# A graph-attention layer whose residual is added in DRAM by accumulating transfers from Pool

## The reference

```
h = jnp.maximum(_layernorm(x, axis=-1), 0.0)
...
h_src = h[src]
h_tgt = h[tgt]
att_in = jnp.concatenate([h_src, h_tgt, e], axis=-1)
att = jnp.sum(att_in * a, axis=-1)
att = jnp.where(att > 0, att, 0.2 * att)
m = jnp.maximum(segment_max(att, tgt), 0.0)
ex = jnp.exp(att - m[tgt])
denom = segment_sum(ex, tgt) + (num_edges - deg)[:, None] * jnp.exp(-m)
h_prime = segment_sum((ex / denom[tgt])[:, :, None] * h_src, tgt)
...
x = x + h_prime
```

## Time and profile before

| | |
|---|---|
| median of 3 runs | 2291.24 us (2289.3 to 2291.45) |
| the profiled execution: its time | 2286.65 us |
| the profiled execution: its span | 2284.8 us |
| Pool busy | 1676.3 us (73%) |
| VectorE busy | 1597.1 us (70%) |
| TensorE busy (matmul) | 1208.8 us (53%) |
| ScalarE busy | 602.1 us (26%) |
| transfers | 199.98 MB, mean 88 GB/s |

### The profile page before, as it was taken

How to read it: one execution, slowest core, us unless ns; L and a number is a source line. 1 busy time by engine, 2 the same in 40 slices (tenths; PEclk the granted TensorE clock), 3 DMA queues, 4 the chain that set the end, 5 groups by cost and what they waited for, 6 DMA issues and landing times. The chain is left out here.

```text
span 2284.8 us, 29035 instructions
## 1 busy us (share of the span) xinstructions
PE 1208.8 (53%) x8459; PEld 1009.0 (44%) x8461; DVE 1597.1 (70%) x4440; ACT 602.1 (26%) x1139; POOL 1676.3 (73%) x1778
## 2 busy tenths in 40 slices
PE   4655555555555555555555554555554554544441
PEld 3514444444444444444444443444444444444441
DVE  7317776767777677776777677676767776777677
ACT  3412222222222222222222222222222222222220
POOL 7877777777777777777777777777777777777740
PEclk8976776777776767776766677777767676666665
DMA  3463233323323233232333333232232322223223
GB/s 120 137 215 98 75 93 80 94 75 86 86 74 98 75 98 75 74 99 74 95 78 84 84 78 94 74 98 74 74 99 75 80 56 56 54 55 86 55 81 145
DMA packets 87796, 199.98 MB, mean 88 GB/s; under 512 B 30142, under 2 KB 49502, under 8 KB 81240
## 3 DMA queue, kind: packets, MB, share of 16 engines
q0 software_dynamic: 53120, 112.30, 21.2%
q1 hardware_dynamic: 32631, 79.28, 10.4%
q10 hardware_dynamic: 1888, 6.56, 0.7%
HBM read 181.70 MB, written 16.31 MB: 87 GB/s over the span
## 5 line engine op out<-in xcount | busy, mean ns | idle before, releaser
L698 POOL DMA_INDIRECT gath<-node_table,src_i x1660 | 1580.5, 952 | 511.5 <-issue 492.4
L778 PE MATMUL bank<-vals,onehot 128*128 128x137 f32 x3328 | 693.1, 386 | 595.2 <-DVE vals L1043 364.9
L778 PEld LDWEIGHTS bank<-vals,onehot 128*128 128x128 f32 x3328 | 643.1, 283 | 620.1 <-DVE vals L1043 375.5
L1077 DVE TENSOR_TENSOR acc<-acc,bank 128x137 f32 x1664 | 495.7, 298 | 426.4 <-PE bank L778 157.3
L853 ACT COPY onehot_t<-ps_oht 128x2048 bf16<-128x2048 bf16 x104 | 194.1, 1866 | 1008.4 <-PE ps_oht L748 984.2
L748 PE MATMUL ps_oht<-ident_b,onehot_b 128*128 128x128 bf16 x1664 | 177.7, 292 | 328.1 <-DVE onehot_b L929 328.1
L862 ACT CAST onehot<-onehot_b 128x384 f32<-128x384 bf16 x624 | 268.7, 474 | 254.3 <-PE bank L778 246.8
L748 PEld LDWEIGHTS ps_oht<-ident_b,onehot_b 128*128 128x128 bf16 x1664 | 161.3, 138 | 336.6 <-DVE onehot_b L929 332.4
L1039 DVE TENSOR_TENSOR vals<-gath,bank 128x2048 f32<-128x2048 f32 x104 | 237.2, 2281 | 1.9 <-ACT bank L866 1.7
L929 DVE TENSOR_TENSOR onehot_b<-bank,rel_s 128x2048 bf16<-128x2048 f32 x104 | 237.1, 2282 | 0.0
L730 PE MATMUL bank<-eattr,w_eatt 128*32 128x512 f32 x392 | 184.5, 615 | 8.0 <-DMA eattr<-edge_attr_in 6.6
(11 more groups left out here) (176 smaller groups left out, 964.9 us busy)
## 6 DMA issues: line engine op xcount, KB each, us to landing
eattr<-edge_attr_in SPq DMA_DIRECT2D x49, 1024.0 KB, 5.7
gath<-node_table,src_i POOLq DMA_INDIRECT x1660
node_table<-onehot_b SPq DMA_DIRECT2D x14, 462.0 KB, 4.0
gath<-x_in SPq DMA_DIRECT2D x14, 448.0 KB, 4.9
gath<-x_in SPq DMA_DIRECT2D x4, 896.0 KB, 5.5
out_dram<-gath ACTq DMA_DIRECT2D x4, 896.0 KB, 3.6
edge_scores<-edge_out SPq DMA_DIRECT2D x49, 64.0 KB, 1.8
edge_s<-edge_scores SPq DMA_DIRECT2D x12, 256.0 KB
```

The costliest lines, as they stand in the source:

```text
L698: nc.gpsimd.indirect_dma_start(out=gath[:, g.r, a * GS + j, :], out_offset=None, in_=table, in_offset=bass.IndirectOffsetOnAxis(ap=src_i[: ...
L778: last = T.matmul(SUM_BANK[b % 3][:, (j % 3) * ACC:(j % 3 + 1) * ACC], onehot[:, b % 3, j % 3, :], vals[:, j, :], start=True, stop=True)
L1077: V.tensor_tensor(a_blk, a_blk, SUM_BANK[(j // 3) % 3][:, (j % 3) * ACC:(j % 3 + 1) * ACC], ALU.add).then_inc(s["added"], 1)
```

## The change

The change does five things.

1. SP no longer loads x again into SBUF. At groups 26, 29, 32, 35, 38, 41 and 44 of the loop it issues instead a transfer from DRAM to DRAM, piece n of x to piece n of the output.
2. In stage 3 VectorE only multiplies, and writes each piece into a buffer of its own (`results[g]`, the same places that `x_again[g]` had). The scratch tile, the seven additions and the waits between them are gone.
3. ACT's seven stores are gone.
4. Pool waits once for the seven copies, and then for each piece it waits for the multiply and issues a transfer from SBUF to the output in DRAM that adds to what stands there (`accum_op=ALU.add`).
5. The semaphores follow.

```diff
-        EARLY = 5
...
-        x_again = [ea_flat[:, 0:FLAT], ea_flat[:, FLAT:2 * FLAT], gath_flat[:, 0:FLAT], gath_flat[:, FLAT:2 * FLAT],
+        results = [ea_flat[:, 0:FLAT], ea_flat[:, FLAT:2 * FLAT], gath_flat[:, 0:FLAT], gath_flat[:, FLAT:2 * FLAT],
...
-        s_again = [sem(f"x_again{g}") for g in range(N_OUT)]
+        out_g = out.rearrange("p (g n) -> g p n", n=FLAT)
+        s_copied = sem("x_copied_to_out")
...
-                        if g.n == NG - 3:
-                            sp.wait_ge(s["edge_ps"], NTG)
-                            for n in range(2):
-                                sp.dma_start(x_again[n], x_out[n, :, :]).then_inc(s_again[n], 16)
-
-                    def finish(g):
-                        sp.wait_ge(s["vals"], 2 * g.n)
-                        for n in range(2, EARLY - 1):
-                            sp.dma_start(x_again[n], x_out[n, :, :]).then_inc(s_again[n], 16)
-                        sp.wait_ge(s["cast"], 2 * NB * g.n)
-                        sp.dma_start(x_again[EARLY - 1], x_out[EARLY - 1, :, :]).then_inc(s_again[EARLY - 1], 16)
-
-                    iterations(sp, start, body, finish)
+                        if g.n >= NG // 2 and (g.n - NG // 2) % 3 == 0 and (g.n - NG // 2) // 3 < N_OUT:
+                            n = (g.n - NG // 2) // 3
+                            sp.dma_start(out_g[n, :, :], x_out[n, :, :]).then_inc(s_copied, 16)
+
+                    iterations(sp, start, body, lambda g: None)
...
-                @block.sync
-                def _(sp):
-                    for g in range(EARLY, N_OUT):
-                        sp.dma_start(x_again[g], x_out[g, :, :]).then_inc(s_again[g], 16)
-
-                @block.scalar
-                def _(act):
+                @block.gpsimd
+                def _(pool):
+                    pool.wait_ge(s_copied, 16 * N_OUT)
                     for g in range(N_OUT):
-                        act.wait_ge(s_y, g + 1)
-                        act.dma_start(out_g[g, :, :], x_again[g]).then_inc(s_out, 16)
-                    act.wait_ge(s_out, 16 * N_OUT)
+                        pool.wait_ge(s_y, g + 1)
+                        pool.dma_start(out_g[g, :, :], results[g], accum_op=ALU.add).then_inc(s_out, 16)
+                    pool.wait_ge(s_out, 16 * N_OUT)
...
                     for g in range(N_OUT):
-                        V.tensor_tensor(y.rearrange("p b (h c) -> p b h c", h=HEADS), a_all[:, g * OW:(g + 1) * OW, :, 0:HD],
-                                        den3[:, g * OW:(g + 1) * OW, :].unsqueeze(3).broadcast_to((P, OW, HEADS, HD)), ALU.mult).then_inc(s_m, 1)
-                        dve.wait_ge(s_m, g + 1)
-                        dve.wait_ge(s_again[g], 16)
-                        V.tensor_tensor(x_again[g], y_flat, x_again[g], ALU.add).then_inc(s_y, 1)
-                        dve.wait_ge(s_y, g + 1)
+                        V.tensor_tensor(results[g].rearrange("p (b h c) -> p b h c", b=OW, h=HEADS), a_all[:, g * OW:(g + 1) * OW, :, 0:HD],
+                                        den3[:, g * OW:(g + 1) * OW, :].unsqueeze(3).broadcast_to((P, OW, HEADS, HD)), ALU.mult).then_inc(s_y, 1)
```

More of the change, by code:

```diff
@@ L1118, in ssb @@
                 return stage.enter_context(nc.sbuf_tensor(name, shape, dt))
-            y = oh_flat[:, G * P // 2:G * P // 2 + FLAT].rearrange("p (w d) -> p w d", w=OW)
             y_flat = oh_flat[:, G * P // 2:G * P // 2 + FLAT]
@@ L1123, in gat_kernel @@
             den3, inv3 = (t.rearrange("p (b h) -> p b h", h=HEADS) for t in (den, inv))
-            s_e, s_d, s_r, s_m, s_y, s_out = (ssem(n) for n in ("empty_nodes", "denominators", "reciprocals", "normalised", "results", "stored"))
-            out_g = out.rearrange("p (g n) -> g p n", n=FLAT)
+            s_e, s_d, s_r, s_y, s_out = (ssem(n) for n in ("empty_nodes", "denominators", "reciprocals", "results", "added_to_out"))
             with nc.Block() as block:
-                @block.sync
-                def _(sp):
-                    for g in range(EARLY, N_OUT):
-                        sp.dma_start(x_again[g], x_out[g, :, :]).then_inc(s_again[g], 16)
-                @block.scalar
-                def _(act):
+                @block.gpsimd
+                def _(pool):
+                    pool.wait_ge(s_copied, 16 * N_OUT)
                     for g in range(N_OUT):
-                        act.wait_ge(s_y, g + 1)
-                        act.dma_start(out_g[g, :, :], x_again[g]).then_inc(s_out, 16)
-                    act.wait_ge(s_out, 16 * N_OUT)
+                        pool.wait_ge(s_y, g + 1)
+                        pool.dma_start(out_g[g, :, :], results[g], accum_op=ALU.add).then_inc(s_out, 16)
+                    pool.wait_ge(s_out, 16 * N_OUT)
                 @block.vector
```

## The result

The changed kernel takes 2294.92 us at the median of 19 runs (2292.59 to 2297.96), the kernel before 2291.31 us of 19 (2288.04 to 2294.58). The ratio is 1.0016, with a 95% interval of 1.0009 to 1.0022: 3.6 us more, inside the 4.6 us that the prediction called no change, and, with this many runs, clear of 1.

A forecast was written before the change was run, and what follows sets the result against it. Loop bound by Pool's issuing (change 0), stage 3 by the transfers: 2255.8 + 7 x 4.73 + 0.9 = 2289.8 against 2284.8, so +5.0 us on 2291.24, 2296.2 us; range 2281 to 2326.

The forecast's parts named there:

- the 4.6 us that the prediction called no change: Whole kernel: about 0.2%, the smallest difference in time that a measurement was taken to tell from no change.
- VectorE's 14.5 us: Stage 3: without the seven adds VectorE ends at 2266.3 instead of 2280.82, a gain only if the transfers can use it.
- the loop's 0: Gather loop: seven copies added and seven x loads removed cost 0 us, hidden by Pool's issuing pace.
- The prediction's sign for a loop that is held: Gather loop: longer VectorE waits on gathers at groups with copies would show copies holding it; rival +33 us, chance 0.02.
- X: Stage 3: engine time per adding transfer, forecast as 2.23 store plus 2.50 load, 4.73 us; span end at 2256.7 + 7X.
- the level case: Stage 3 rival: reads partly overlap or load start-up is paid once, X 3.36 to 4.67, time the same; chance 0.31.
- the ends: Stage 3: first data at 2255.8, 0.94 issue plus 0.8 us behind the first multiply; 0.9 us after the last data.
- the price of a copy: Loop: each DRAM-to-DRAM copy moves one load and one store's worth of bytes, about 4.7 us of the transfer engines.
- slower by over 0.2%: Whole kernel: outcome with X above 4.67, or copies holding the loop; chance 0.57.
- the hidden second read: Stage 3 rival: second read hidden beside first read and write, 2.23 us a piece, -12.5 us, 2278.7; chance 0.12.
- the gathers' queue pace: Stage 3 rival: both streams at the loop pace of Pool's queue, 7.9 us a piece, +27.3 us, 2318.5; chance 0.19.
- the row-by-row case: Stage 3 rival: each row read, added and written before the next, 13.6 us a piece, +67 us, 2358; chance 0.09.

The follow-up runs named there:

- the copies alone: Kernel before with only the seven DRAM-to-DRAM copies added to its loop, stage 3 unchanged: 2289.09 us against 2287.51, ratio 1.0001.
- the plain-store kernel: Changed kernel with plain stores from Pool in place of the adding transfers, x left out of the output: 2279.23 us against 2287.51, ratio 0.9954, stage 3 26.7 us.

## Why the prediction came out as it did

**Right: what the time hangs on.** VectorE's 14.5 us were to be given back because the transfers end last; they were. VectorE finished 18.9 us into the stage, the stage took 42.1, and the plain-store kernel shows that without the additions 15.4 us of it would have gone.

**Right within about 2 us: the loop's 0.** Pool's pace is unchanged, and the copies alone give 1.0001 (0.9992 to 1.0010). An effect of up to about 2 us can't be excluded. The prediction's sign for a loop that is held, longer waits of VectorE for gathers at the groups with copies, did not show: from 1200 to 1900 us they are 27.1 us in the changed kernel and 30.1 before. Over the whole loop they are 82.1 against 71.6 us, all of the surplus outside that stretch.

**Right in mechanism, mis-sized: X, "2.23 + 2.50 = 4.73 us a piece".** It measured 4.40. The 2.50 us of the load had the wait for the first data in it, and the level case's figure without it, 4.46, came nearer. That the wait is what made the difference is not shown by a run of its own. The ratio to a plain store from the same queue is 4.40 / 2.26 = 1.95. The Trainium skill, "Collectives: The Full Stack", section "The bandwidth ceiling: the fold count and why AG ≠ RS ≠ AR", gives 1.93 for a collective whose transfers add against one whose transfers copy, and as the cause two reads through one queue. The runs agree with the ratio, and show that the price is the same with both operands in SBUF. That the reads share a queue, and that the addition itself is free, is not seen in any profile here.

**Mis-sized: the ends, 0.9 us for the completion and a first issue right behind the multiply.** Data began 9.4 us into the stage instead of 9.0, since Pool starts its issue 0.7 us late and 0.3 us of that is won back (data 1.45 us behind the start of the issue instead of 1.74), and the end came 1.9 us behind the last data instead of 0.9. ACT's row was carried over to Pool's queue, and Pool's is slower by 0.8 to 0.9 us at either end. The terms add up: 9.4 + 30.8 + 1.9 = 42.1, where the prediction had 9.0 + 33.1 + 0.9 = 43.0. The pieces were taken 2.3 us too long and the ends 1.4 us too short, so that part of the agreement is luck.

**Wrong: the price of a copy, "one load and one store's worth of bytes, about 4.7 us".** Without cover it is 2.7. In the sum it counted 0 either way.

**The size of it.** 2296.2 was forecast and 2294.92 measured, and +5.0 us against 3.6. I gave "slower by over 0.2%" the larger chance, and the measured 0.16% lies in the level case, whose X (3.36 to 4.67) holds 4.40. Of the rivals, the hidden second read (2.23), the gathers' queue pace (7.9) and the row-by-row case (13.6) are all refuted by one number, the 4.40 us of a piece.

## What to carry to other kernels

Price a transfer that adds as two plain ones (1.95 here, for float32 in rows of 7168 bytes, with the sum in DRAM or in SBUF), and then ask which engine ends last: an addition moved from VectorE to the transfers saves nothing once they are the longer chain. Where a stage has idle transfer time, move only so many pieces that both chains end together; here two of seven, first in order, gave 0.9986, and 0.9973 with the last piece in halves as well, where seven gave 1.0016. A copy between DRAM tensors can be put under an issue-bound loop at no measurable cost; the same seven copies at the place of use cost 14.3 of their 19.1 us, the rest being hidden under VectorE's own start of the stage.

## What was unexpected of the hardware

One chip ran the kernel before at 3353.34 us instead of 2290, and the others likewise. Its chain of waits (engine, what waited, for whom: us, times, longest), in the kernel with plain stores from ACT:

```profile
ACT onehot_t L844 <- remote: 1286.3, 49, 35.0
DVE acc L1068 <- PE bank L769: 1149.0, 181, 18.4
POOL gath L689 <- DVE vals L1034: 641.0, 50, 49.7
```

Pool, which waits for almost nobody elsewhere, waits there for VectorE, which waits for TensorE, and ScalarE's copies wait up to 35 us for something that the profile only calls remote. What it is stays open; the gathers' own 944 ns and stage 3 are the same on both chips. The mean granted clock of TensorE was lower there (0.64 against 0.71 to 0.72), but TensorE's busy time grew only from 1209 to 1296 us, far less than the 1060 us that are missing.

The multiplies, once no wait stood between them, followed each other at 1.94 us although each shows 2.02: by the profile VectorE starts one before the last has ended.
